# First mixer of a fused image network: products grouped per tile, norms shared by two engines, VectorE's work in another order

## The reference, cut to what matters

```python
def _mix_w(x, W1, b1, W2, b2):            # _mix_h is the same along the other axis
    y = jnp.einsum('bhwd,ed->bhwe', x, W1) + b1
    y = jnp.transpose(y, (0, 3, 2, 1)).reshape(b_, -1, H)
    z = _grouped_mix(y, W2, b2, SEG)
    attn = jax.nn.softmax(z.reshape(b_, Wd, Wd, H).transpose(0, 3, 1, 2), axis=-1)
    return jnp.einsum('bhij,bhjd->bhid', attn, x)
...
Y = Y_h + Y_w + (jnp.einsum('bhwd,od->bhwo', x, Wc) + bc)
return jnp.einsum('bhwd,od->bhwo', Y, Wo) + bo
...
x = x + _L0_conv_ref(_ln_c(x), ...)
t = t + _L0_ffn_ref(_ln_t(t), ...)
```

## Time and profile before

| | us |
|---|---|
| median of 3 runs | 2193.96 |
| lowest and highest run | 2189.43, 2201.25 |
| the profiled execution, its own time | 2195.41 |
| its span, first to last instruction | 2193.4 |

### The profile page before, as it was taken

How to read it: one execution, slowest core, us unless ns; L and a number is a source line. 1 busy time by engine, 2 the same in 40 slices (tenths; PEclk the granted TensorE clock), 3 DMA queues, 4 the chain that set the end, 5 groups by cost and what they waited for, 6 DMA issues and landing times.

```text
span 2193.4 us, 65534 instructions
## 1 busy us (share of the span) xinstructions
PE 1866.8 (85%) x25858; PEld 1458.6 (66%) x25858; DVE 1575.9 (72%) x5073; ACT 1133.2 (52%) x2217; POOL 1284.8 (59%) x1350
## 2 busy tenths in 40 slices
PE   3869687059999993999999999999999927999997
PEld 2546454047777773788777877777778625777775
DVE  4374755437877775777889888898989745777775
ACT  3323320047777773565555554555554206777775
POOL 3225444647787773554556564656665673777776
PEclk9565655579999996999999998999999758999998
DMA  9201000326555547000000000000000024555553
GB/s 153 77 26 48 13 24 23 131 80 211 181 180 194 187 152 116 3 4 3 3 5 11 10 11 10 11 10 11 11 11 11 12 94 127 189 184 193 184 188 100
DMA packets 95797, 174.94 MB, mean 80 GB/s; under 512 B 53618, under 2 KB 66955, under 8 KB 95492
## 3 DMA queue, kind: packets, MB, share of 16 engines
q10 hardware_dynamic: 21312, 102.00, 13.9%
q1 hardware_dynamic: 56516, 42.48, 8.5%
q0 software_dynamic: 17664, 26.27, 3.6%
HBM read 135.33 MB, written 37.31 MB: 79 GB/s over the span
## 4 chain that ended last, share of the span: by engine, by line
PE 58%; DVE 24%; issue 7%; POOL 4%; ACT 4%; DMA 1%; DVEq 0%; SPq 0%; ACTq 0%; POOLq 0%
PE ps L1062 10%; PE ps L1063 9%; PE ps L1064 9%; PE ps L1143 6%; PE ps L1031 4%; PE ps L1178 3%; PE ps L1033 3%; PE ps L1192 2%; PE ps L1102 2%; POOL rows L585 2%; PE ps L981 2%; PE ps L1074 2%; ACT rounded L859 1%; PE ps L1214 1%; PE ps L1189 1%
## 5 line engine op out<-in xcount | busy, mean ns | idle before, releaser
L1062 PE MATMUL ps<-rounded 97*128 97x512 f32 (+2 forms) x952 | 394.2, 414 | 4.1 <-DVE rounded L1824 2.8
L1063 PE MATMUL ps<-rounded 97*128 97x512 f32 (+2 forms) x952 | 377.1, 396 | 0.0
L1064 PE MATMUL ps<-rounded 97*128 97x512 f32 (+2 forms) x952 | 377.0, 396 | 0.0
L1143 PE MATMUL ps<-rounded 128*128 128x224 f32 (+1 forms) x2256 | 352.8, 299 | 4.4 <-ACT rounded L859 4.4
L838 ACT ACTIVATE rounded<-ps 128x512 fp32r<-128x512 f32 x444 | 267.1, 602 | 162.1 <-PE ps L1064 153.9
L1143 PEld LDWEIGHTS ps<-rounded 128*128 128x128 f32 x2256 | 307.0, 200 | 39.3 <-issue 10.3
L1859 DVE TENSOR_TENSOR rounded<-arena,rounded 128x512 fp32r<-128x512 f32 x296 | 224.6, 759 | 135.4 <-ACT arena L839 135.2
L605 POOL TENSOR_TENSOR rounded<-arena,rounded 128x512 fp32r<-128x512 f32 x148 | 192.7, 1302 | 161.3 <-ACT arena L839 156.5
L839 ACT ACTIVATE arena<-ps 128x512 f32<-128x512 f32 x444 | 267.0, 601 | 0.0
L673 POOL TENSOR_TENSOR w<-arena,consts 128x384 f32<-128x384 f32 x128 | 107.8, 842 | 220.0 <-DVE arena L1354 220.0
L1062 PEld LDWEIGHTS ps<-rounded 97*128 97x128 f32 (+2 forms) x952 | 166.8, 175 | 57.3 <-issue 10.4
(11 more groups left out here) (317 smaller groups left out, 3940.9 us busy)
## 6 DMA issues: line engine op xcount, KB each, us to landing
rounded<-weights_by_expert ACTq DMA_DIRECT2D x148, 673.0 KB, 4.6
arena<-rows SPq DMA_DIRECT2D x74, 208.0 KB, 2.6
residual<-in_x SPq DMA_DIRECT2D x16, 384.0 KB, 7.2
weights_by_expert<-rounded SPq DMA_DIRECT2D x8, 672.0 KB, 3.2
residual<-after_ffn SPq DMA_DIRECT2D x12, 384.0 KB, 6.9
after_ffn<-arena POOLq DMA_INDIRECT x148
out<-arena POOLq DMA_INDIRECT x148
w<-in_w SPq DMA_DIRECT2D x4, 576.0 KB
```

The source lines that it names most:

```text
L1062: pe.matmul(dst, left[0], right[0], start=start, stop=False)
L1063: pe.matmul(dst, left[1], right[0], start=False, stop=False)
L1064: return pe.matmul(dst, left[0], right[1], start=False, stop=stop)
L1143: pe.matmul(dst[:, 0:w], x3[:, x_part, n, slot, tokens], wtap[:, w_part, n, y + 1, 0:w], start=(y == 0 and n == x_part == w_part == 0), st ...
```

## The change

Seven edits, all in the first mixer:

1. In `mix_rows` the four full-array products of a tile come first and then its sixteen 32 x 32 blocks. Only the first product of a tile opens the PSUM bank.
2. Of group 0, ACT norms the even tiles and DVE the odd ones (`odd_tiles`); PE transposes a tile as soon as it is there, and ACT norms tiles 2, 4 and 6 between its copies.
3. DVE turns the column result (`turn_columns`) ahead of the row additions, not behind them; the addition stands between tiles 5 and 6.
4. `gated` and `placed` move between the additions: after tiles 0 and 1, and after tiles 2 and 3. PE's `ranks_of` follows tile 3, not tile 1.
5. `row_sums` of a group stands at the end of its own turn; it stood between the softmaxes of the next group. `next_sums` stands ahead of `values`, not behind it, and `kept_std` between the softmaxes.
6. ACT norms the next group's rows ahead of `gate_exp` (20 of the 32 from group 1 on).
7. POOL's list follows: `powers` of group g + 1 behind 22, 22 and 16 scatters of group g, `norm_of(3)` behind `powers(1)`, the weights 4 to 7 together behind `norm_of(2)`.

```diff
             for g in range(G):
-                cuts = (22, 26) if g == 0 else (26, 26) if g == 1 else (16, 16)
-                scatter_group(g, range(0, cuts[0]))
+                cut = (22, 22, 16, SIDE)[g]
+                scatter_group(g, range(cut))
+                if g + 1 < G:
+                    powers(g + 1)
                 if g == 0:
                     norm_of(3)
-                scatter_group(g, range(*cuts))
-                if g + 1 < G:
-                    powers(g + 1)
-                scatter_group(g, range(cuts[1], SIDE))
+                scatter_group(g, range(cut, SIDE))
...
             def columns_and_values(g):
                 for q in range(NQ + 2):
+                    if g == 0 and q % 2 == 1 and q < NQ - 1:
+                        normalise(0, range(Q * (q + 1), Q * (q + 2)))
...
-                for i in range(Q):
-                    h, dst = Q * q + i, bank(2 + q % 2)[:, i * DS:(i + 1) * DS]
-                    pe.matmul(dst, xt0[0:D + 1, h * P:(h + 1) * P], rhs0[0:D + 1, VC:NV], start=True, stop=False)
+                tile_rows = [(Q * q + i, bank(2 + q % 2)[:, i * DS:(i + 1) * DS]) for i in range(Q)]
+                for h, dst in tile_rows:
+                    pe.matmul(dst, xt0[0:D + 1, h * P:(h + 1) * P], rhs0[0:D + 1, VC:NV], start=(h == Q * q), stop=False)
+                for h, dst in tile_rows:
                     for pb in quarter:
-                        ins = pe.matmul(dst[pb, :], at[pb, 1, :, h], vc[pb, h, 0:DS], start=False, stop=True)
+                        ins = pe.matmul(dst[pb, :], at[pb, 1, :, h], vc[pb, h, 0:DS], start=False, stop=(h == Q * q + Q - 1))
...
             def next_sums(g):
-                dve.wait_ge(m_ln, NQ * g)
+                dve.wait_ge(m_ln, NQ * g - NQ // 2)
                 sums_of_rows(g)
+
+            def odd_tiles():
+                for q in range(1, NQ, 2):
+                    for h in range(Q * q, Q * q + Q):
+                        ins = dve.tensor_scalar(xn[:, h, :], xr[:, 0, h, :], moments[:, 5, h:h + 1], moments[:, 1, h:h + 1], ALU.mult, ALU.add)
+                    ins.then_inc(m_ln_odd, 1)
...
-                if g:
-                    row_sums(g - 1)
+                if g + 1 < G:
+                    kept_std(g + 1)
                 shares(g, 1)
+                turn_columns(g)
+                add_rows(g, range(2))
                 if g:
                     gated(g - 1)
-                add_rows(g, range(2))
+                add_rows(g, range(2, 4))
                 if g:
                     placed(g - 1)
-                add_rows(g, range(2, NQ))
-                add_columns(g)
+                add_rows(g, range(4, 6))
+                add_columns(g, 6)
+                add_rows(g, range(6, NQ))
+                dve.wait_ge(m_w_add, (g + 1) * NQ)
+                row_sums(g)
+                if g + 2 < G:
+                    next_sums(g + 2)
                 if g + 1 < G:
                     values(g + 1)
-                if g + 2 < G:
-                    next_sums(g + 2)
```

More of the change, by code:

```diff
@@ L308, in metaformer @@
         tables_in = [sem(f"tables_in{l}") for l in range(2)]
-        mix2_in = sem("mix2_in")
+        mix2_in, m_ln_odd = sem("mix2_in"), sem("m_ln_odd")
         m_ln, m_t_pe, m_t_ev, m_h_pe, m_h_ev = (sem(n) for n in ("m_ln", "m_t_pe", "m_t_ev", "m_h_pe", "m_h_ev"))
@@ L739, in _, with normalise @@
         def _(act):
-            def normalise(g):
+            def normalise(g, rows_=range(SIDE)):
                 act.wait_ge(rstd_ready, g + 1)
                 need(act, m_t_pe, g * NQ)
-                for h in range(SIDE):
+                for h in rows_:
                     ins = act.activation(xn[:, h, :], xr[:, g, h, :], ACT.Identity, bias=moments[:, 1, h:h + 1], scale=moments[:, 5, h:h + 1])
@@ L774, in gate_exp @@
                 act.activation(ge[:, :, :], gd[:, :, :], ACT.Exp).then_inc(rt["exp"], 1)
-            normalise(0)
+            normalise(0, range(Q))
             columns_and_values(0)
@@ L785, in _ @@
                     mixed_columns(g, q)
+                if g + 1 < G:
+                    normalise(g + 1, range(20 if g else SIDE))
                 if g:
@@ L788, in _ @@
                 if g + 1 < G:
-                    normalise(g + 1)
+                    if g:
+                        normalise(g + 1, range(20, SIDE))
                     columns_and_values(g + 1)
@@ L964, in to_columns @@
                 k = g * NQ + q
-                pe.wait_ge(m_ln, k + 1)
+                if g:
+                    pe.wait_ge(m_ln, k + 1 - NQ // 2)
+                else:
+                    pe.wait_ge(m_ln_odd if q % 2 else m_ln, q // 2 + 1)
                 if g and q == 0:
@@ L1052, in _ @@
                     mix_rows(g, q)
-                    if q == 1 and g:
+                    if q == 3 and g:
                         ranks_of(g - 1)
@@ L1671, in add_rows, with turn_columns, add_columns @@
                     dve.tensor_tensor(rows, rows, bank(2 + q % 2)[:, 0:Q * DS].rearrange("p (a b) -> p a b", b=DS), ALU.add).then_inc(m_w_add, 1)
-            def add_columns(g):
-                dve.wait_ge(m_w_add, (g + 1) * NQ)
+            def turn_columns(g):
                 dve.wait_ge(m_h_ev, (g + 1) * NQ)
-                ch.link(dve.transpose(ohw[:, :, :].rearrange("p h d -> p d h"), oh[:, :, :].rearrange("p w d -> p d w")))
+                ch.done(dve.transpose(ohw[:, :, :].rearrange("p h d -> p d h"), oh[:, :, :].rearrange("p w d -> p d w")))
+            def add_columns(g, added):
+                dve.wait_ge(m_w_add, g * NQ + added)
+                ch.wait()
                 ch.link(dve.tensor_tensor(xsc[:, g, :, :], xsc[:, g, :, :], ohw[:, :, :], ALU.add))
@@ L1780, in _ @@
             kept_std(0)
+            odd_tiles()
             next_sums(1)
@@ L1790, in _ @@
                 below_peaks(g, 1)
-                if g:
-                    row_sums(g - 1)
+                if g + 1 < G:
+                    kept_std(g + 1)
                 shares(g, 1)
+                turn_columns(g)
+                add_rows(g, range(2))
                 if g:
                     gated(g - 1)
-                add_rows(g, range(2))
+                add_rows(g, range(2, 4))
                 if g:
                     placed(g - 1)
-                add_rows(g, range(2, NQ))
-                add_columns(g)
+                add_rows(g, range(4, 6))
[5 more added lines that the diff above has]
+                    next_sums(g + 2)
                 if g + 1 < G:
                     values(g + 1)
-                if g + 2 < G:
-                    next_sums(g + 2)
             dve.sem_inc(stage_end, 1)
-            row_sums(G - 1)
             gated(G - 1)
```

6 lines of the change are left out of this document (2 added, 4 removed).

## The result

The changed kernel takes **2106.28 us** (2098.34 to 2108.75, 4 runs), the kernel before beside it 2193.86 (2189.43 to 2201.25): ratio 0.9591, 95% interval 0.9554 to 0.9629. The forecast was 2111, faster. The profiled execution took 2104.41, its span is 2102.4.

A forecast was written before the change was run, and what follows sets the result against it. PE held 58% of the chain and bounded row mixing, DVE the way from values through column mixing, POOL's scatters the end. Terms summed to 83.9 us off 2195.4, giving 2111.5, said as 2111; own range 2106 to 2117, wider 2093 to 2133.

The forecast's parts named there:

- First norms, 7.7: Start of group 0: ACT and DVE share the norms, so its values start at 45.3 in place of 53.0, 7.7 us gained.
- Row mixing of group 0, 9.6 + 7.5: Grouped tiles at 3.42 us gain 9.6; the clock rising after 11 us, with tiles 3 to 7 at 1.93, gains 7.5.
- Group 1, 11.9: Group 1's row mixing ends 28.9 us after t, DVE's last softmax transpose, in place of 40.8: 11.9 us gained.
- group 2, 9.7: Group 2's row mixing takes 28.9 us in place of 38.6, at PE's lower clock: 9.7 us gained.
- rival 2: The clock rises in every group's row mixing, DVE then bounds groups 1 and 2: about 2101 us, or 2094; chance 0.22.
- From row mixing to the next column mixing, 6.2 + 6.2 + 0: next_sums leaves the way behind values: 21.2 us becomes 15.0 in groups 1 and 2, 12.4 us together.
- From column to row mixing, 3 x 3.0: row_sums leaves the way between softmaxes: 11.7 us becomes 8.7 in groups 1, 2 and 3, 9.0 us together.
- End, 16.1: Last scatters: POOL's idle time of 21.1 us for group 3's sums goes, later slots lose 5.0; net 16.1 us gained.
- rival 3: Grouping gives nothing because the 0.42 us lies in the blocks; 38.7 us of row mixing gain goes: 2150 us; chance 0.08.
- rival 5: Slower than before: DVE's turns and copies hold up POOL's scatters; at 3.9 us a scatter 2280 us; chance 0.01.
- rival 1: The clock stays down in all row mixing, so the 7.5 us of group 0 is missing: 2118 us; chance 0.18.
- rival 4: Moved waits do not hide (addition 2 behind gates, norm_of(3) late, instruction gap), 2 to 4 us a group: 2125 us; chance 0.15.

The follow-up runs named there:

- experiment 3: Changed kernel with a tile's products grouped by two rows, not four: tiles 3.85 us apart at the lower clock, 2.24 at the higher; single time 2204.88 us, not used.
- experiment 1: Kernel before with only the grouping of each tile's products (four full products, then sixteen blocks): 2158.31 us, ratio 0.9858; on another chip ratio 0.9915.
- split_turn: Changed kernel with 10, not 22, group 0 scatters before the roots and DVE's turn in four parts, one ahead of each of additions 0 to 3: 2181.79 us, ratio 0.9546.
- experiment 4: Changed kernel repeated (2109.25 us, ratio 0.9635), and with 10, not 22, group 0 scatters ahead of group 1's root and group 3's norm (2102.44 us, 0.9613; second chip 0.9668).
- experiment 6: Changed kernel with row_sums back between the softmaxes, next_sums behind values and POOL's norm ahead of its root: 2238.44 us, ratio 0.9778.
- root_early_2: Changed kernel with 10, not 22, scatters of group 0 ahead of group 1's root and group 3's norm: 2102.44 us, ratio 0.9613.

## Why the prediction was right

The sum was 83.9 us and 89.9 came, at the last scatter. Term by term, forecast and then measured, from the stage starts of both traces:

- **First norms, 7.7:** 9.75 (53.03 to 43.28). DVE's norms take 0.25 us each, and PE's clock is up from about 30 us.
- **Row mixing of group 0, 9.6 + 7.5:** 11.0. The price of a tile was right (3.42 said, 3.45 measured; 1.93 and 1.91), and so was the 0.42 per pair of changes (experiment 3). The step on the clock failed in its mechanism: I let the stage begin at the lower clock and rise after 11 us. It began at the higher and fell after PE's wait, and then 17.3 us of unbroken grouped work (76.2 to 93.5) did not raise it. Of the 11.0, 9.8 are the grouping at the lower clock (experiment 1); two tiles and part of a third at the higher clock gave some 4 us, and the 2.80 of wait took most of that back. I had written that the turn ahead of the additions costs PE nothing "at the lower clock"; at the higher it costs the wait and, as split_turn shows, with it about 10 us of the stage.
- **Group 1, 11.9:** 17.6, **group 2, 9.7:** 9.5. Group 1 went by rival 2's account: tiles 0, 1 and most of 4 to 7 at the higher clock, end at 23.1 where I had 28.9. Group 2 took 29.1 us at clock 0.50, as forecast, but that was luck: it began low after a wait that the prediction had excluded, POOL's late norm, and took 23.2 where that wait was gone (experiment 4). (Rival 2's own terms, 12 less 2 and 2, give 2103, not the 2101 that stands there.)
- **From row mixing to the next column mixing, 6.2 + 6.2 + 0:** 7.2, 10.1 and 1.5. 6.4 of each of the first two is next_sums (experiment 6). Most of the rest, 0.6 and 3.4, is the columns and values, which PE does at clock 0.93 and 0.95 in place of 0.85 and 0.66; the prediction had nothing for this. The cover was as thin as said: PE's part lasts 12.4 us in group 1, and DVE then bounds it.
- **From column to row mixing, 3 x 3.0:** 3.0, -0.3 and 2.9. This is the step that failed on the ledger of waits: `norm_of(3)`, "free, by 2 us". I had DVE ask for it 60 us after group 1's t and POOL done at 57.8. With t at 130.5 DVE asked at 183.8, 53.3 after it, mostly since group 1's row mixing was 5.8 us shorter than forecast, and POOL was done at 190.1, 59.6 after it, with one scatter 2.2 us longer than the others. DVE waited 6.38 us, 3.3 of them on the path (7.8 us from L1668 to L1672, in group 1 4.5), and the clock of the row mixing behind it was lost with it. Not in the sum was group 0's: 12.5 to 9.0, 3.5 gained, since the stop of 3.62 us before 79.14 is gone.
- **End, 16.1:** 14.1. The slots came 18.4 us after the start of the row mixing and POOL idled for nothing but its root, both as said. POOL took 88.6 us for 86.6, for one scatter of 3.43 us beside DVE's column addition.

So the time came out near by luck in part: errors cancel, the clock of group 0 (6.1 too much) and of group 1 (5.7 too little), the 3.4 short between column and row mixing and the 3.5 won at the stop. The 6 us more than the sum are what came unforeseen between a row mixing and the next column mixing (6.4, most of it at the columns and values) and at the first norms (2.1), less 2.0 at the end. Rivals 3 and 5 are refuted, 1 and 2 each hold in some groups, 4 at one place. Shown by experiment are the price of the changes of shape, the grouping's 37 us by itself (38.7 in the terms, which also hold the new order in groups 1 and 2), the 22 us of the sums in their stretches, the norm's wait, and that in group 0 the wait behind the turn brings the clock down: it fell in all six traces that have this wait after a start at the higher clock (2.13 to 3.30 us), and stayed up in the three where products fill it or the turn is split. That the wait for the norm sets the clock of group 2's row mixing rests on two traces at either side. What raises the clock within a row mixing stays open: it rose behind the ranks of groups 1 and 3 (145.7 in group 1, after 8 us at the lower), not in group 0 and not behind those of group 2, and in root_early_2 not in group 1 either.

## What to carry to other kernels

Price a change of tile shape on TensorE from two neighbouring rows, and check it with an intermediate grouping: here the cost went by the number of changes, at both clocks. A short wait of TensorE can cost several times its length when the clock comes down with it for the rest of a stage: 2.8 us of wait cost 10.5 in group 0. So an operation of another engine ahead of what TensorE waits for is worth pricing even where it looks hidden. But look where the wait goes: splitting the turn won 10.5 us in group 0 and lost 3.9 and 4.5 in groups 1 and 2, where it came back behind the gates. When a stage gets shorter, go again through every step that was hidden by a margin of a few microseconds: the one with 2 us of margin was the one that came out.

## What the hardware did that I had not expected

**A scatter is held up by an addition of two SBUF operands.** POOL's and DVE's timelines of the changed kernel in group 1:
```profile
150.55 0.96 POOL L585 DMA_INDIRECT rows<-residual,arena  x1 [0.30 <-issue]
151.82 3.13 POOL L585 DMA_INDIRECT rows<-residual,arena  x1 [0.31 <-issue]
```
```profile
150.62 3.49 DVE L1691 TENSOR_TENSOR residual<-residual,arena 128x3200 f32<-128x3200 f32 x1
```
The scatter that began inside the addition ends 0.84 us after it (154.95, 154.11) and took 3.13 us for 0.96; the one that had begun 0.07 us ahead of it took its 0.96. The same in groups 2 (3.55) and 3 (3.43), and beside no turn and no statistics. The kernel before had it too, where the prediction did not look: its scatter at 302.26 took 3.97 us and ended 0.84 us after the column addition (301.90 to 305.39), and the two ahead of it, beside the turn, took 0.96 each. A shorter product of two SBUF operands does it in small: the changed kernel's scatter at 249.21 the first behind a root, took 1.75 us and ended 0.90 after DVE's step of 1.23 us at 248.83; the first behind the next root, at 306.72, took 1.20. The Trainium skill, SBUF — State Buffer, section SBUF: two separate sides, says that a DVE operation with two SBUF inputs and a GpSimd operation that reads SBUF exclude each other for the whole instruction, and whichever starts first has it; the rows agree, if a scatter counts as such an operation, which that passage does not say. That is rival 5's mechanism, but for one scatter in each of three groups, 2.2 to 2.6 us longer, and not for 64 of them.

**The clock's level is carried in.** The same stage took 15.3 or 27.6 us in two runs of one kernel, on two chips, and group 2's row mixing 23.2 or 29.1 on one chip. Unbroken work at the lower clock did not raise it in 37.4 us of alternating shapes, nor in 27.6 and 29.1 us of grouped ones. The Trainium skill, TensorE: Matmul & The Clock Gate, Part 1, says that sustained activity releases the clock. Group 1 of the changed kernel agrees (up at 145.7 us, after 8 us at the lower clock), these stages do not.
